# Normalizations of a transformer's feed-forward and output: scaled on ACT instead of DVE, with contraction, combine and value projections of a pass in another order

## What is computed

```python
for i in range(DEPTH):                      # 6
    x = attn_layer(shift_tokens(x), Wqkv[i], q_scale[i], k_scale[i], Wo[i]) + x
    x = ffn_layer(shift_tokens(x), ln_g[i], ln_b[i], W1[i], b1[i], W2[i], b2[i]) + x
...
def ffn_layer(x, g, bln, W1, b1, W2, b2):
    mu = x.mean(-1, keepdims=True)
    var = ((x - mu) ** 2).mean(-1, keepdims=True)
    xn = (x - mu) / jnp.sqrt(var + 1e-05) * g + bln
    hg = xn @ W1 + b1
    a, gate = jnp.split(hg, 2, -1)
    return a * jax.nn.gelu(gate, approximate=False) @ W2 + b2
```

## Time and profile before

| | |
|---|---|
| median of 3 runs | 4029.53 us |
| the profiled execution's own time | 4028.28 us |
| its span | 4026.2 us |
| PE busy | 3753.8 us (93%) |
| DVE busy | 3116.4 us (77%) |
| ACT busy | 2174.9 us (54%) |
| POOL busy | 2360.0 us (59%) |
| TensorE clock granted in the span | 0.98 |

### The profile page before, as it was taken

One profiled execution on the slowest core, in us unless ns is written; L12 is line 12 of the kernel. 1 busy time (PEld: TensorE's weight loads), 2 busy tenths in 40 slices (PEclk: granted clock), 3 DMA queues, 4 the chain that ended last, 5 costly groups with the idle time before them and its releaser, 6 DMA issues.

```text
span 4026.2 us, 149129 instructions
## 1 busy us (share of the span) xinstructions
PE 3753.8 (93%) x67429; PEld 2616.8 (65%) x67429; DVE 3116.4 (77%) x5129; ACT 2174.9 (54%) x3263; POOL 2360.0 (59%) x1644
## 2 busy tenths in 40 slices
PE   5999999986899999999999999999999999998887
PEld 3776777664566666666666666666666666665555
DVE  4434544455888888898898898998888889899994
ACT  3111111043566666666667666766766676665653
POOL 2001000015777777777777777777777777776662
PEclk8999999998999999999999999999999999999997
DMA  4111111000000000000000000000000000000000
GB/s 163 43 43 64 43 43 56 29 1 6 9 11 11 13 26 22 12 12 16 21 25 11 11 24 21 17 12 12 21 21 19 12 11 23 27 13 15 14 12 12
DMA packets 50654, 98.35 MB, mean 24 GB/s; under 512 B 11611, under 2 KB 40678, under 8 KB 45542
## 3 DMA queue, kind: packets, MB, share of 16 engines
q1 hardware_dynamic: 49286, 88.42, 7.0%
q10 hardware_dynamic: 736, 0.40, 0.0%
HBM read 61.25 MB, written 2.36 MB: 16 GB/s over the span
## 4 chain that ended last, share of the span: by engine, by line
PE 50%; DVE 13%; DMA 5%; issue 5%; ACT 3%; SPq 1%; POOL 1%; DVEq 0%; POOLq 0%
PE pQ L1725 12%; PE pC L1823 6%; PE pW L1748 6%; PE pW L1707 5%; PE pM L1788 4%; DMA ys<-XT 4%; PE pW L1788 4%; PE pM L1774 3%; PE pW L1763 3%; DVE m L1439 3%; PE pW L1774 3%; DVE rot L1429 3%; DVE PT L1419 2%; DVE sm L1409 1%; ACT sq L1584 1%
## 5 line engine op out<-in xcount | busy, mean ns | idle before, releaser
L1316 POOL TENSOR_TENSOR rot<-rot,m 128x1024 f32<-128x1024 f32 x384 | 908.3, 2365 | 319.8 <-DVE m L1439 319.8
L1308 POOL TENSOR_TENSOR rot<-rot,rn 128x1024 f32<-128x1024 f32 x384 | 729.2, 1910 | 7.5
L1584 ACT ACTIVATE sq<-pQ 128x1024 f32<-128x1024 f32 x380 | 389.6, 1025 | 586.7 <-PE pQ L1725 570.7
L1451 DVE TENSOR_REDUCE n<-sq 128x16 f32<-128x1024 f32 x380 | 461.3, 1214 | 147.4 <-ACT sq L1584 146.2
L1429 DVE TENSOR_TENSOR rot<-pQ,tabl 128x1024 f32<-128x1024 f32 x380 | 462.9, 1218 | 101.7 <-ACT sq L1584 101.6
L1439 DVE TENSOR_TENSOR m<-pQ,tabl 128x1024 f32<-128x1024 f32 x380 | 458.4, 1206 | 4.0 <-POOL rot L1316 4.0
L597 POOL TENSOR_TENSOR b_xcT<-b_cB,b_xT 128x2048 f32<-128x2048 f32 x16 | 72.2, 4516 | 605.0 <-DMA b_cB<-b_crow 605.0
L1725 PE MATMUL pQ<-wq,xs 128*128 128x512 f32 x760 | 380.4, 623 | 18.8 <-DVE m L1439 15.4
L1725 PE MATMUL pQ<-wk,xs 128*128 128x512 f32 x760 | 380.4, 623 | 13.7 <-DVE m L1439 8.1
L1345 POOL TENSOR_TENSOR E<-E,rc 128x1024 f32<-128x1024 f32 x192 | 361.9, 1909 | 9.0 <-DVE rc L1411 9.0
L1748 PEld LDWEIGHTS pW<-PT,V 32*64 32x64 f32 x24576 | 291.1, 131 | 100.2 <-issue 99.3
(11 more groups left out here) (238 smaller groups left out, 6883.5 us busy)
## 6 DMA issues: line engine op xcount, KB each, us to landing
b_cB<-b_crow SPq DMA_DIRECT2D x32, 1024.0 KB, 6.1
xs<-XT SPq DMA_DIRECT2D x192, 64.0 KB, 2.7
ys<-XT SPq DMA_DIRECT2D x192, 64.0 KB, 2.0
wq<-in_wqkv SPq DMA_DIRECT2D x6, 512.0 KB, 3.7
wk<-in_wqkv SPq DMA_DIRECT2D x6, 512.0 KB, 5.0
wv<-in_wqkv SPq DMA_DIRECT2D x6, 512.0 KB, 4.8
wo<-in_wo SPq DMA_DIRECT2D x6, 512.0 KB, 4.8
w<-in_w SPq DMA_DIRECT2D x6, 384.0 KB, 4.1
```

What stands on the lines that cost most here:

```text
L1308: e.tensor_tensor(r, r, rn[b % 2][:, c:c + HEADS].unsqueeze(2).to_broadcast([P, HEADS, HD]), ALU.mult)\
L1316: e.tensor_tensor(rot[j % RING][:, :], rot[j % RING][:, :], m2[:, :, :].rearrange("p h d -> p (h d)"), ALU.add)\
L1451: e.tensor_reduce(n2[:, c:c + HEADS], heads(squared(j)), AX.X, ALU.add).then_inc(v_red.sem, 1)
L1584: e.activation(squared(j), projected(j), ACT.Square).then_inc(a_sq.sem, 1)
```

## The change

The scaling of both norms moves from DVE to ACT, as `Identity` with a scale and a bias of each partition; POOL forms the bias as minus mean times root, in two small instructions each (`mean_shift`, and the end of `last_root`). POOL also adds epsilon for the final norm, which DVE did. On PE, `back` goes behind the three first value projections and a `turn`, the fourth value projection goes ahead, `contract` goes ahead of `combine`, and `last` goes ahead of most of the pass. The streams of ACT, DVE and POOL are reordered with it; the number of table loads on ACT is the same.

```diff
-    MOVES = "v0 v1 v2 t0a t0b t1b t1a v3 t3a t2a t2b t3b".split()
+    MOVES = "v0 v1 v2 t1a t0b v3 t0a t1b t3a t2a t2b t3b".split()
...
+            def mean_shift(n):
+                if n is None:
+                    return
+                e.wait_ge(g_c.sem, g_c.at("rs", n))
+                e.tensor_tensor(my[:, :], mv[:, :, 0], yr[:, :], ALU.mult).then_inc(g_c.sem, 1)
+                e.wait_ge(g_c.sem, g_c.at("my", n))
+                e.tensor_scalar(sh[:, :], my[:, :], -1.0, None, ALU.mult).then_inc(g_c.sem, 1)
...
             def last_root(n):
...
+                e.tensor_scalar(fve[:, :], fmv[:, :, 1], EPS, None, ALU.add).then_inc(g_f.sem, 1)
+                e.wait_ge(g_f.sem, g_f.at("ve", f))
                 power_rsqrt(e, g_f, fyr[:, :], fve[:, :], yh[:, :])
+                e.wait_ge(g_f.sem, g_f.at("rs", f))
+                e.tensor_tensor(fmy[:, :], fmv[:, :, 0], fyr[:, :], ALU.mult).then_inc(g_f.sem, 1)
+                e.wait_ge(g_f.sem, g_f.at("my", f))
+                e.tensor_scalar(fsh[:, :], fmy[:, :], -1.0, None, ALU.mult).then_inc(g_f.sem, 1)
...
                 root(C)
+                mean_shift(C)
                 rotary_add(A, 0)
...
                 rotary_add(A, 1)
+                by_sum(B, 0)
                 unit_scale(R, 2)
                 last_root(F)
                 rotary_add(A, 2)
-                by_sum(B, 0)
                 by_sum(B, 1)
...
-                    e.tensor_scalar(xh[:, t, :], pC[:, L + t * P:L + (t + 1) * P], mv[:, t, 0:1], yr[:, t:t + 1],
-                                    ALU.subtract, ALU.mult).then_inc(v_c.sem, 1)
...
-                    e.tensor_scalar(X[:, f, t, :], X[:, f, t, :], fmv[:, t, 0:1], fyr[:, t:t + 1], ALU.subtract, ALU.mult)\
-                        .then_inc(v_f.sem, 1)
...
-                normal(C)
+                last_stats(F)
                 squares(A, 1)
...
+                    e.activation(xh[:, t, :], pC[:, L + t * P:L + (t + 1) * P], ACT.Identity, bias=sh[:, t:t + 1], scale=yr[:, t:t + 1])\
+                        .then_inc(a_c.sem, 1)
...
+                    e.activation(X[:, f, t, :], X[:, f, t, :], ACT.Identity, bias=fsh[:, t:t + 1], scale=fyr[:, t:t + 1])\
+                        .then_inc(a_f.sem, 1)
```

More of the change, by code:

```diff
@@ L1185, in transformer_phase @@
         fyr = sb("fyr", [P, T])
+        fmy = sb("fmy", [P, T])
+        fsh = sb("fsh", [P, T])
         pQ = ps("pQ", [P, N])
@@ L1501, in last_stats @@
                 e.wait_ge(v_f.sem, v_f.at("add", f))
+                if f:
+                    e.wait_ge(g_f.sem, g_f.at("sh", f - 1))
                 layernorm_stats(e, v_f, f, lambda t: X[:, f, t, :], fst, fmv, "")
[L1503 to L1511, removed]
-                    e.tensor_scalar(X[:, f, t, :], X[:, f, t, :], fmv[:, t, 0:1], fyr[:, t:t + 1], ALU.subtract, ALU.mult)\
-                        .then_inc(v_f.sem, 1)
             e.wait_ge(const_l, 64)
@@ L1527, in _ @@
                 less_max(B, 1)
-                last_stats(F)
+                sums(B, 0)
+                hidden(C, 0)
                 cosines(A, 2)
-                hidden(C, 0)
+                hidden(C, 2)
+                sines(A, 2)
+                hidden(C, 1)
                 squares(A, 2)
[L1532 to L1535, removed]
                 sums(B, 1)
-                last_normal(F)
-                squares(A, 3)
+                probs(B, 0)
                 cosines(A, 3)
-                probs(B, 0)
                 sines(A, 3)
+                probs(B, 1)
                 attention_add(Dn)
                 ffn_add(C)
-                probs(B, 1)
+                squares(A, 3)
         @block.scalar
@@ L1659, in _ @@
                 gelu(C, 1)
-                values(R, 3)
+                turned(R, "1b")
                 square(A, 2)
+                turned(R, "0a")
                 gelu(C, 2)
                 exponents_again(C)
-                exponent(B, 0)
+                last_normal(F)
                 exponent(B, 1)
@@ L1849, in _ @@
                 project(A, 0)
-                back(C)
                 values(R, 0)
@@ L1853, in _ @@
                 values(R, 2)
+                turn(R, "1a")
+                back(C)
+                turn(R, "0b")
+                project(A, 1)
+                last(F)
                 scores(B, 1, 0)
-                project(A, 1)
+                values(R, 3)
                 turn(R, "0a")
-                turn(R, "0b")
-                scores(B, 1, 1)
                 normed(C)
                 turn(R, "1b")
-                turn(R, "1a")
+                scores(B, 1, 1)
                 hidden(C, 0)
-                last(F)
-                values(R, 3)
                 project(A, 2)
@@ L1875, in _ @@
                 turn(R, "2b")
+                contract(C)
+                turn(R, "3b")
                 combine(Dn)
-                turn(R, "3b")
-                contract(C)
 def layout(i):
```

61 lines of the change are left out of this document (37 added, 24 removed).

## The result

The change is slower: 4080.75 us (median of 4 runs, 4077.81 to 4083.73) against 4029.07 for the kernel before in runs beside it. The ratio is 1.0133, 95% interval 1.0118 to 1.0147. The profiled execution took 4080.67 us, its span is 4078.7. The forecast of 4023 and its range up to 4056 were both missed, on the slow side.

What follows compares the result with a forecast made beforehand. PE was taken to bound passes without F, another engine (DVE's final-norm steps) the 11 with F. Terms -34 + 21 + 4 + 3 = -6 took 4028.28 to 4022.3, forecast 4023 us; own range 4006 to 4040, with rivals 3998 to 4056.

Steps and rivals of the forecast that it cites:

- (d): Passes with F: DVE relieved, but ACT's final norm waits for POOL, about 5 us in one piece; +3 us, bounds -4 and +8.
- (c): Layer starts: wv is issued later, behind the later attention_add; five times 0.7, +4 us, bounds 0 and 9.
- (a): Full passes: back's wait for ys goes as back starts later; saves 34 us, bounds 27 to 36.
- (b): Every pass: PE newly waits at hidden 0 for ACT and at hidden 2 for the first product; +21 us, bounds 5 to 40.
- rival 2: The new waits of (b) are taken up by PE's existing waits in the weighted values: 5 not 21, total 4007; chance 0.17.
- Rival 1: Passes with F fall to the others' length, 34.3 to 30.8 us, 35 us off, total 3985; chance 0.1.
- Rival 3: ACT becomes what a pass waits for: both new PE waits total 0.65 per pass, 53 us, total 4058; chance 0.2.
- Rival 4: The wait for ys does not go, so the -34 falls away, total 4057; chance 0.05.

Runs made afterwards that it cites:

- E6: E5 with ACT taking the third GELU ahead of a turned copy of queries instead of behind it: 3983.42 us, ratio 0.9897.
- E7: E4 plus, on ACT, the copy of a turned key piece ahead of the mask and two copies reordered, norms still on DVE: 3997.06 us, ratio 0.9929.
- E9: Kernel before with E7's order and copies, wv loaded early, final norm on ACT with early root, feed-forward norm on DVE: 3948.89 us, ratio 0.9797.
- E5: The change with both the final norm's root earlier on POOL and wv loaded ahead of the ys copies: 3978.58 us, ratio 0.9883.
- E8: E5 with the feed-forward norm scaled on DVE again and no POOL shift for it: 3976.99 us, ratio 0.9873.
- E2: The change with SP issuing the next layer's wv load ahead of the ys copies: 4067.26 us, ratio 1.0086.
- E1: The change with POOL forming the final norm's root and shift earlier, before the refinement of the norms' roots: 4015.4 us, ratio 0.996.
- E3: The change with nine unused PE matmuls added in passes with F, where PE stands still: 4079.69 us, ratio 1.012.
- E4: Kernel before with only PE's order changed, back behind three value projections and contract ahead of combine: 4069.09 us, ratio 1.0087.

## Why the prediction was wrong

Between the forecast difference of -6 us and the span's +52.5 lie 58.5: 23.6 in (d), 12.2 in (c), 10.6 in (a) and (b) together, 8.9 at the end, and 3.2 ahead of the first pass.

**(a) The wait for `ys`** was right: no `back` waits for it in full passes, and a typical ordinary pass is 0.45 shorter, 68 x 0.45 = 31 us, with (b) in it. That this is near the 34 forecast for (a) alone is luck: with (b) the forecast was 13.

**(b) The two new waits** were too dear. In the full pass without `F` that starts at 2583.00, `hidden` 0 starts 5.83 behind the second projection. ACT's `xnT` is done 5.74 behind it, as forecast; PE was slower to get there than its summed prices of 5.43, as the prediction suspected, and does not wait. `hidden` 2 is reached 1.70 behind the weighted values instead of 1.52: this wait is there, with the size that was forecast (0.16), but E6 takes it away and gains nothing. Of the 21 us forecast little can be seen, so rival 2 was right on that point. But the sum of the ordinary passes did not follow the typical pass: 68 passes gained 2.4 us, not 31. PE's idle time in them did fall by 15.2 us (69.2 to 54.0), and its busy time rose by 12.8. Some 3.5 of that is the clock: the stretches at half clock add up to 32.6 us instead of 25.5. One of the long passes by busy time and granted clock (us, PE, PEld, DVE, ACT, POOL busy, PEclk, DMA share, GB/s), before:

```profile
1245.14:1277.75 32.61, 30.09 (x665) 20.72 (x665) 27.21 (x35) 20.97 (x31) 23.08 (x17) 1.00 0.04 11
```

and in the change:

```profile
1248.79:1284.70 35.91, 33.24 (x666) 22.19 (x665) 26.86 (x34) 21.98 (x33) 24.27 (x20) 0.90 0.04 10
```

PE stalls for 2.5 us in this pass before and 2.4 in the change without a named engine; what is new is the half clock behind the stall. These stalls are not longer in the change (29.1 us in the 68 passes, 30.0 before). From 1000 us on there are 12 of over 1 us before and 15 in the change, and by the DMA records of the traces every one ends 1.2 to 1.6 us after a transfer has landed in the queue that the page lists as `q8 instruction`, where one lands every 6 us on average. So they look like waits for PE's own instructions, which no run tests. The other 9 us of busy time stay open. E7 and E9 show that an order with the same contraction and `back` gets 28 to 30 us out of the same passes; which of the other moved calls of the change costs it that was not taken apart. It is not the norm's place: E5 and E8 have the same 2082.

**(c) Layer starts** were mis-sized: +4 forecast (at most 9), +16.2 measured. The later issue was right (0.57 against 0.7). Left out were that `back`, with its wait, had been standing ahead of the values as cover, and the half clock behind a wait of over 3 us. The waits for `wv` make up 7.5 of the 16.2, and there are 17.1 us at half clock instead of 3.4. E2 settles it: with the load early these 15 passes are 18.5 us shorter. That is more than these passes move by themselves: E1 and E3, which do not touch them, have 6.0 and 7.4 more than the change.

**(d) The passes with `F`** is the step that failed, and in a narrow place. The walk from the first projection held to 0.3 us:

| | forecast | measured |
|---|---|---|
| refinement of the norms' roots starts | 12.79 | 12.61 |
| second scaling and `E<-E,rc` done, epsilon starts | 22.35 | 22.28 |
| shift formed | 23.95 | 23.92 |
| second exponent starts | 24.65 | 24.75 |
| PE's `turn` goes | 27.06 | 27.32 |
| next pass's first projection | 34.7 | 37.56 |

Up to the wait the error is 0.3 us; behind it 10.24 us stand where 7.65 were taken from a pass at full clock. "It waits in another place, about 5 us in one piece" was written down and priced as if 5 us in one piece cost no more than the same time spread over many waits; its clock was not thought of. E3 gives the size, 2.5 us per pass, and E1 the whole of it, wait and clock: 37.56 to 30.25. At full clock, as in E3, the ten passes would have been 8.7 us longer than before, just above the bound of +8; with the clock's 17.9 they are 26.6 longer, 18.6 above it.

The end of the program, +8.9 us, was no term of the sum at all: the last units run with the same wait of ACT. From 3933 us PE waits 8.9 us there for `oT`, in two places, and E1's end is 134.1.

**The rivals.** None came as told. Rival 1 (passes with `F` at 30.8) is what E1 shows, 30.25; its condition, "ACT's wait to be covered", was what decided. Rival 3 said slower, but by waits for ACT in every pass, and these did not come. Rival 4 did not come either: no wait for `ys` is left. The advice of the Trainium skill to keep products and sums off ScalarE (ScalarE: Activation LUTs, Rules for kernel authors) found no support here: E8 against E5 is no difference, with the two 128-column scalings at 0.80 us a pass on ACT.

**The ranges.** The bounds of (b) and (d) at a half give 4011 to 4035, not the 4006 to 4040 of the prediction; the result lies far outside both.

## What to carry to other kernels

A wait that has moved is not a wait that has kept its price: many short ones gathered into one long one ahead of PE's work can cost the clock on top, so the calls behind a wait of several microseconds should be priced from rows at the lower clock too. When work moves to another engine, ask first where its inputs are made in the producer's stream; here one group of small POOL instructions, moved up by five calls, was worth 65 us, and moving the scaling of the other norm nothing. A reordering on one engine has to be carried through on the engine that returns its buffers (E4 against E7), and through the queue of the loads (E2).

## What was not expected of the hardware

The granted clock fell to 0.50 for 6.8 us after a wait of 4.8 us in a pass that is otherwise dense, and it did so behind that wait in 8 of ten passes (for 3.4 us in one of them); a `turn` then took 1.09 instead of 0.60 and three value projections 5.28 instead of 2.8 us, while the combine, mostly run after the clock was back, took 3.75 instead of 3.62. At a layer start 3.4 us of waiting had the same effect. In an ordinary pass a stall of 2.1 us was followed by 6.8 us at half clock too, while others of about 2 us were not. The two 128-column scalings on ACT take 457 ns each, below the 0.564 us of the 256-column form, and the small POOL instructions on two columns 196 to 254 ns, both close to what was assumed.
